# A graph attention pass: the three parts of the queries from one matmul of 192 columns, added by VectorE

## The chip, the cores and the metric

One core of a Trainium2 chip. The metric is the device time of one execution in microseconds; of several, the median. The profile is of one execution, with its own time. Its engines are PE (TensorE), DVE (VectorE), ACT (ScalarE), POOL (GpSimd) and SP (SyncE).

## The reference

A graph of 12500 nodes with 128 features and 412500 edges (200000 random pairs in both directions, and a loop for each node), sorted. Cut to what matters:

```python
q = (X @ Wq)[src]; k = (X @ Wk)[dst]          # 64 columns each
e = jnp.tanh(q + k)
scores = e @ Wphi
exp_scores = jnp.exp(scores - jnp.max(scores))
denom = segment_sum(exp_scores, src)
alpha = exp_scores / (denom[src] + 1e-09)
msg = alpha[:, None] * ((X @ Wy_w + Wy_b)[dst] + e @ We)
out = layernorm(X + segment_sum(msg, src), axis=-1)
```

## The kernel before

The nodes stand in 98 blocks of 128. The first parts of the kernel make a table in HBM with a row per node (64 columns of k, 128 of x), keep the queries of all nodes in SBUF as `q3` (per block three bf16 parts of 64 columns each, whose sum is the f32 query), and sort the edges so that each tile of 128 edges has all its sources in one block. Then comes the main part, in which the change lies, and at the end the normalization.

The main part is one pass over the tiles of edges, 16 to a chunk and four to a step ("quad", `q` in the code); it has 206 chunks, 824 steps. The code of each engine is written out step by step, software-pipelined by hand, with semaphores that count steps. For step q:

- SyncE loads, once a chunk, the numbers of the sources within their block, broadcast to all partitions (L1060, 512 KB); it may be up to two chunks ahead of the one-hots (L1059).
- GpSimd gathers the table rows of the step, four indirect DMAs of 128 rows (L1085), into one of five slots of `gathered`. It waits until the sums of the step five before are made (L1082). Every 72nd step (18 chunks are a "period") is not gathered by it but brought by SyncE, row by row: 512 single-row copies (L1073), 32 in each of 16 chunks of the period, with row numbers read into registers (L1069). Before the first of them SyncE waits for the sums of the last step of the period before (L1067). There are 11 such periods; the last chunks have no such copies.
- VectorE builds once a chunk the one-hots of the sources, transposed (`src_onehots_T`, L1154) and straight (L1157).
- TensorE makes the queries of the step's edges (L1109): the transposed one-hot is the weights, and the three bf16 parts of the block's queries are the moving operand. The three matmuls of a tile add up in PSUM; the four tiles lie side by side in bank 0 or 1 (`QK`), by turns.
- VectorE adds the gathered k (L1168, one instruction for the four tiles) into columns ROW to ROW+A of the slot; ScalarE takes the tanh in place (L1129); VectorE multiplies by phi and reduces (L1176, L1178); ScalarE takes the exponential (L1134) and scales the one-hots with it (L1140).
- TensorE makes the sums of the step (L1120, f32, four matmuls of 193 columns, which the profile shows as eight), three steps behind the queries, into banks 4 to 7; VectorE adds them to the sums of the blocks (L1192, four instructions).

Within one step VectorE's order is: one-hots (every fourth step), L1168 of q-1, L1176 and L1178 of q-2, four L1192 of q-4. TensorE's is: queries of q, sums of q-3. TensorE's queries of step q wait until L1168 of q-2 has read the bank (L1103). A few of the last chunks stand in branches, since their number depends on the data.

Of the kernel before, what the change touches and what calls it, by code (L numbers as in the profile page):

```python
# [4 lines left out]
PARTS = 128  # L5
COLS = 64
UNIT = 16
QUAD = 4
# [24 lines left out]
def gnn_program(nc, x, src, dst, Wq, Wk, Wphi, Wy_w, Wy_b, We, out):  # L33
    f32, i32, u32 = mybir.dt.float32, mybir.dt.int32, mybir.dt.uint32
    bf16, f16 = mybir.dt.bfloat16, mybir.dt.float16
    ALU, ACT, AX = mybir.AluOpType, mybir.ActivationFunctionType, mybir.AxisListType
# [3 lines left out]
    A = Wq.shape[1]  # L40
# [5 lines left out]
    ROW = A + D  # L46
# [37 lines left out]
    def sb(where, name, shape, dt):  # L84
        return where.enter_context(nc.sbuf_tensor(name, shape, dt))

    def sem(name):
        return ctx.enter_context(nc.semaphore(name))

    with ctx:  # L90
        bank = [ctx.enter_context(nc.psum_tensor(f"bank{i}", [PARTS, 512], f32)) for i in range(8)]
# [17 lines left out]
        q3 = sb(ctx, "q_parts", [PARTS, NB * 3 * A], bf16)  # L109
# [11 lines left out]
        def spread(col, n, m):  # L121
            return col.rearrange("p (a m) -> p a m", a=1).to_broadcast([PARTS, n, m])
# [753 lines left out]
        slot = sb(lists, "gathered", [PARTS, RING + 1, QUAD, SLOT], f32)  # L876
# [3 lines left out]
        ohT = sb(lists, "src_onehots_T", [PARTS, 2, CHUNK * PARTS], bf16)  # L880
# [87 lines left out]
        def tensor_lists(e):  # L968
# [3 lines left out]
            for n, i in enumerate(LOADS):  # L972
# [5 lines left out]
                for j in range(min(4, NR - i)):  # L978
# [3 lines left out]
        gathered = [sem(f"gathered_{i}") for i in range(RING)]  # L982
        rows_by_sync = [sem(f"rows_by_sync_{i}") for i in range(4)]
        lows_loaded = [sem(f"src_in_block_rows_loaded_{i}") for i in range(LOB)]
        sums_cleared_vector = sem("sums_cleared_vector")
        onehots_made, onehots_T_made = sem("src_onehots_made"), sem("src_onehots_T_made")
        queried, added_qk, tanh_made = sem("queried"), sem("added_qk"), sem("tanh_made")
        times_phi, scored, weights_made, weighted = sem("times_phi"), sem("scored"), sem("weights_made"), sem("weighted")
        totalled, accumulated = sem("totalled"), sem("accumulated")
# [1 line left out]
        steps_over = {k: sem(f"steps_over_{k}") for k in ENGINES}  # L991
        arrive = {k: sem(f"pass_over_{k}") for k in ENGINES if k != "sync"}
        leave = {k: sem(f"pass_next_{k}") for k in ENGINES if k != "sync"}
        pass_sems = [*gathered, *rows_by_sync, *lows_loaded, sums_cleared_vector, onehots_made, onehots_T_made, queried, added_qk, tanh_made,
                     times_phi, scored, weights_made, weighted, totalled, accumulated, row_max, core_max, shift_made, eps_made, *steps_over.values()]
        QK, SM = [bank[0], bank[1]], [bank[4], bank[5], bank[6], bank[7]]
        H3 = NB * SUMS // 3
        NC = NTS // CHUNK
        SURE = min(NC, -(-NT // CHUNK))
# [16 lines left out]
        def slot_of(q):  # L1016
            return RING if by_sync(q) else pool_no(q) % RING

        def wait_for_rows(e, q):
            if by_sync(q):  # L1020
                e.wait_ge(rows_by_sync[q // PERIOD % 4], 16 * STEP_ROWS * (q // PERIOD // 4 + 1))
            else:
                e.wait_ge(gathered[pool_no(q) % RING], 16 * QUAD * (pool_no(q) // RING + 1))
# [4 lines left out]
        def load_blocks(e, regs, which, t):  # L1028
            p_, c_ = t // MAPC, t % MAPC
            e.load(regs, bmap[p_:p_ + 1, which, c_:c_ + CHUNK])  # L1030
# [63 lines left out]
        def tensor_steps(e, regs, first, end, limit):  # L1094
            for step in range(first, end):
                q = step
                if q < limit:
                    c = q // QUADS_PER_CHUNK
                    if q % QUADS_PER_CHUNK == 0:
                        load_blocks(e, regs, 0, q * QUAD)  # L1100
                    e.wait_ge(onehots_T_made, c + 1)
                    if q >= 2:
                        e.wait_ge(added_qk, q - 1)  # L1103
                    for j in range(QUAD):
                        t = q * QUAD + j
                        o = t % CHUNK * PARTS
                        b = e.snap(regs[t % CHUNK], min_val=0, max_val=(NB - 1) * 3 * A)
                        for s_ in range(3):
                            made = e.matmul(QK[q % 2][:, j * A:(j + 1) * A], ohT[:, c % 2, o:o + PARTS], q3[:, bass.ds(b + s_ * A, A)],  # L1109
                                            start=s_ == 0, stop=s_ == 2)  # L1110
                    made.then_inc(queried, 1)
                q = step - 3
                if 0 <= q < limit:
                    r = slot_of(q)
                    e.wait_ge(weighted, q + 1)
                    if q >= 2:
                        e.wait_ge(accumulated, (q - 1) * QUAD)
                    for j in range(QUAD):
                        o = j % 2 * SUMS
                        made = e.matmul(SM[q % 2 * 2 + j // 2][:, o:o + SUMS], ohw[:, q % 3, j, :], slot[:, r, j, A:SLOT], start=True, stop=True)  # L1120
                    made.then_inc(totalled, 1)
# [21 lines left out]
        def vector_steps(e, regs, first, end, limit):  # L1143
            if first == 0:
                if SURE < NC:
                    e.memset(score[:, SURE * CHUNK:NTS], -1e30)
            for step in range(first, end):
                q = step
                if q < limit and q % QUADS_PER_CHUNK == 0:
                    c = q // QUADS_PER_CHUNK  # L1150
                    e.wait_ge(lows_loaded[c % LOB], 16 * (c // LOB + 1))
                    if c >= 2:
                        e.wait_ge(queried, (c - 1) * QUADS_PER_CHUNK)
                    e.tensor_scalar(ohT[:, c % 2, :], lob[:, c % LOB, :], part0[:, :], None, ALU.is_equal).then_inc(onehots_T_made, 1)  # L1154
                    if c >= 2:
                        e.wait_ge(weighted, (c - 1) * QUADS_PER_CHUNK)
                    e.tensor_tensor(oh[:, c % 2, :, :, :], lo[:, c * CHUNK:(c + 1) * CHUNK].rearrange("p (q a j) -> p q a j", a=1, j=QUAD)  # L1157
                                    .to_broadcast([PARTS, QUADS_PER_CHUNK, PARTS, QUAD]),
                                    row1c[:, :, :].rearrange("p (a n) j -> p a n j", a=1).to_broadcast([PARTS, QUADS_PER_CHUNK, PARTS, QUAD]),
                                    ALU.is_equal).then_inc(onehots_made, 1)  # L1160
                if step < 3:
                    e.memset(sums[:, step * H3:(step + 1) * H3 if step < 2 else NB * SUMS], 0.0).then_inc(sums_cleared_vector, 1)
                q = step - 1
                if 0 <= q < limit:
                    r = slot_of(q)
                    e.wait_ge(queried, q + 1)
                    wait_for_rows(e, q)
                    e.tensor_tensor(slot[:, r, :, ROW:ROW + A], QK[q % 2][:, 0:QUAD * A].rearrange("p (j f) -> p j f", f=A), slot[:, r, :, 0:A],  # L1168
                                    ALU.add).then_inc(added_qk, 1)
                q = step - 2  # L1170
                if 0 <= q < limit:
                    r, k = slot_of(q), q % 2
                    e.wait_ge(tanh_made, q + 1)
                    if q >= 2:
                        e.wait_ge(scored, q - 1)
                    e.tensor_tensor(ephi[:, k], slot[:, r, :, ROW:ROW + A], spread(phi[:, :], QUAD, A), ALU.mult).then_inc(times_phi, 1)  # L1176
                    e.wait_ge(times_phi, q + 1)
                    e.tensor_reduce(score[:, q * QUAD:(q + 1) * QUAD], ephi[:, k], AX.X, ALU.add).then_inc(scored, 1)  # L1178
                q = step - 4
                if 0 <= q < limit:  # L1180
                    if q % QUADS_PER_CHUNK == 0:
                        load_blocks(e, regs, 1, q * QUAD)
                    e.wait_ge(totalled, q + 1)
                    if q == 0:
                        e.wait_ge(sums_cleared_vector, 3)
                    for j in range(QUAD):
                        t = q * QUAD + j
                        o = j % 2 * SUMS
                        b = e.snap(regs[t % CHUNK], min_val=0, max_val=(NB - 1) * SUMS)
                        if t:  # L1190
                            e.wait_ge(accumulated, t)
                        e.tensor_tensor(sums[:, bass.ds(b, SUMS)], sums[:, bass.ds(b, SUMS)], SM[q % 2 * 2 + j // 2][:, o:o + SUMS],  # L1192
                                        ALU.add).then_inc(accumulated, 1)
# [311 lines left out]
```

## Time and profile before

| | us |
|---|---|
| median of 3 runs (lowest, highest) | 7010.81 (7007.23, 7012.87) |
| the profiled execution | 7016.36 |
| its span, first to last instruction | 7014.5 |
| busy: PE, DVE, ACT, POOL | 3898.3, 3592.0, 2751.7, 3447.3 |
| main part, from the first L1109 to the last L1120 | 1326.5 to 6917 |

The mean granted TensorE clock is 0.66 of full speed. In the rows of a timeline, the first number is when the work starts, in us from the span's start, the second how long it takes from the first of the instructions to the end of the last, and in brackets stands how long the engine was idle before it and what ended that. "remote" and "issue" are endings for which the profile shows no instruction of the core.

### The profile page before, as it was taken

To read this page: it belongs to the slowest core of one execution; us is meant where nothing else is said; L and a number is where in the kernel's file an instruction comes from. 1 tells how busy PE (TensorE), PEld (TensorE's weight loads), DVE (VectorE), ACT (ScalarE), POOL (GpSimd) and SP (SyncE) were. 2 spreads that over 40 slices of the span, in tenths; PEclk is the share of its full clock that TensorE was granted. 3 is DMA by queue.
4 is the path that set the end of the run, shared out by engine and by line. 5 is a ranking of instruction groups with operands and counts; after the bars stand their busy time and mean duration, and the time that the engine had idled before them with its cause. 6 is when DMAs were issued, how large, how long until landed. Compare 5 with 4: busy or idle time off the path is not lost. (4 is left out here: it accounts for less than half of the span.)

```text
span 7014.5 us, 115608 instructions
## 1 busy us (share of the span) xinstructions
PE 3898.3 (56%) x25925; PEld 2946.3 (42%) x25925; DVE 3592.0 (51%) x8202; ACT 2751.7 (39%) x10900; POOL 3447.3 (49%) x3516
## 2 busy tenths in 40 slices
PE   7899999554544544544444445445445444454456
PEld 6555555343433433433434334334334334343346
DVE  7788888544444444444444444444444444444446
ACT  3788888322322322323223223223223223232235
POOL 1133323455655555655555555555555555555552
PEclk9766666666666666666666666666666666666668
DMA  2100000222322222222222222222222222222234
GB/s 82 45 4 4 5 4 4 62 75 75 84 74 77 80 75 81 80 74 79 77 76 81 76 75 84 74 78 80 79 80 77 75 79 79 75 82 76 76 91 100
DMA packets 288906, 479.68 MB, mean 68 GB/s; under 512 B 96903, under 2 KB 208745, under 8 KB 287988
## 3 DMA queue, kind: packets, MB, share of 16 engines
q0 software_dynamic: 164032, 321.94, 17.4%
q1 hardware_dynamic: 106418, 145.33, 6.5%
q10 hardware_dynamic: 17794, 4.91, 0.3%
q8 instruction: 253, 4.15, 0.2%
q14 instruction: 409, 3.35, 0.2%
HBM read 456.45 MB, written 20.60 MB: 68 GB/s over the span
## 5 line engine op out<-in xcount | busy, mean ns | idle before, releaser
L1085 POOL DMA_INDIRECT gathered<-table,dst_rows x3252 | 3109.2, 956 | 2496.0 <-PE bank L1120 1167.3
L1120 PE MATMUL bank<-gathered,weighted_onehots 128*128 128x193 f32 x6592 | 1939.8, 437 | 997.1 <-issue 677.5
L1120 PEld LDWEIGHTS bank<-gathered,weighted_onehots 128*128 128x128 f32 x6592 | 1519.4, 257 | 1145.2 <-issue 901.7
L1109 PE MATMUL bank<-q_parts,src_onehots_T 128*128 x9888 | 818.0, 215 | 1996.7 <-DVE src_onehots_T L1154 1460.1
L1129 ACT ACTIVATE gathered<-gathered 128x256 f32<-128x256 f32 x824 | 346.3, 420 | 3597.9 <-DVE gathered L1168 3305.6
L1109 PEld LDWEIGHTS bank<-q_parts,src_onehots_T 128*128 128x128 bf16 x9888 | 686.3, 108 | 2271.3 <-issue 2160.6
L1192 DVE TENSOR_TENSOR block_sums<-block_sums,bank 128x193 f32 x3296 | 1169.2, 355 | 637.5 <-issue 198.9
L1140 ACT ACTIVATE weighted_onehots<-src_onehots,edge_weight 128x128 f32<-128x128 bf16 x3296 | 1075.3, 397 | 26.9
L817 ACT ACTIVATE places_past_far<-bank,stat 128x98 bf16<-128x98 f32 x2727 | 884.7, 400 | 129.3 <-DVE place_col L800 58.1
L1168 DVE TENSOR_TENSOR gathered<-bank,gathered 128x256 f32<-128x256 f32 x824 | 345.8, 420 | 1145.3 <-remote 1124.2
L1154 DVE TENSOR_SCALAR src_onehots_T<-src_in_block_rows,partition_number_from 128x2048 bf16<-128x2048 bf16 x206 | 155.2, 754 | 1335.6 <-DMA src_in_block_rows<-src_in_block_list 1280.5
L859 POOL DMA_INDIRECT sorted_list<-sorted_groups,unit_destinations x248 | 317.1, 1279 | 812.0 <-DVE sorted_groups L787 748.1
L817 ACT ACTIVATION_READ_ACCUMULATOR places_past_far<-bank,stat 128x1 f32 x2727 | 705.7, 265 | 0.0
L842 PE MATMUL bank<-block_onehots,before_far 128*128 128x392 bf16 x806 | 408.5, 507 | 0.0
L849 PE MATMUL bank<-col_records,row_onehots 128*128 128x128 f16 x3223 | 402.7, 298 | 4.2 <-DVE col_records L765 4.2
L849 PEld LDWEIGHTS bank<-col_records,row_onehots 128*128 128x128 bf16 x3223 | 380.6, 124 | 29.9 <-issue 24.8
L1134 ACT ACTIVATE edge_weight<-scores,stat 128x4 f32<-128x4 f32 x824 | 245.0, 297 | 308.6 <-DVE scores L1178 211.0
L1178 DVE TENSOR_REDUCE scores<-e_times_phi 128x4 f32<-128x256 f32 x824 | 346.1, 420 | 28.1
L841 PE MATMUL bank<-base_parts_flat,ones 2*128 2x392 bf16 x806 | 348.1, 432 | 17.1 <-DMA base_parts_flat<-base_parts 14.2
L1176 DVE TENSOR_TENSOR e_times_phi<-gathered,phi 128x256 f32<-128x256 f32 x824 | 347.8, 422 | 0.0
L1157 DVE TENSOR_TENSOR src_onehots<-src_in_block,row_to_quad 128x2048 bf16<-128x2048 bf16 x206 | 250.9, 1218 | 0.0
L760 DVE TENSOR_TENSOR row_onehots<-place_row,row_to_sort_chunk 128x3584 bf16<-128x3584 bf16 (+1 forms) x125 | 233.9, 1872 | 0.0
(182 smaller groups left out, 2021.7 us busy)
## 6 DMA issues: line engine op xcount, KB each, us to landing
src_in_block_rows<-src_in_block_list SPq DMA_DIRECT2D x206, 512.0 KB
gathered<-table SPq DMA_DIRECT2D x5632, 0.8 KB
gathered<-table,dst_rows POOLq DMA_INDIRECT x3252
table<-in_x SPq DMA_DIRECT2D x4, 1562.5 KB
x_in<-in_x SPq DMA_DIRECT2D x24, 256.0 KB, 3.0
x_again<-in_x SPq DMA_DIRECT2D x48, 128.0 KB, 2.3
out<-out_rows SPq DMA_DIRECT2D x48, 128.0 KB, 1.9
sorted_list<-sorted_groups,unit_destinations POOLq DMA_INDIRECT x248
```

Source lines behind the costliest of these rows:

```text
L817: made = e.activation(past_far[:, k % 3, j, :], PL[b % len(PL)][:, j * NB:(j + 1) * NB], ACT.Relu, bias=NEAR, accum_out=pos[:, g % 2, t0 + ...
L841: e.matmul(o, ones[0:2, :], flat[:, g % FLATS, t0:t0 + mt, :], start=True, stop=False)
L842: e.matmul(o, before_far[:, :], hot[:, g % 2, c, h0 // PB, :, 0:mt].rearrange("p b t -> p t b"), start=False, stop=True).then_inc(placed, 1)
L849: made = e.matmul(O[:, 0:2 * COLS], hotr[:, k, t // PB, :, t % PB], recc[:, k, :, t // PB, :, t % PB], start=c + t == 0, stop=c * SORT_CHU ...
L1085: e.indirect_dma_start(slot[:, r, j, 0:ROW], None, table, bass.IndirectOffsetOnAxis(ap=gidx[:, t:t + 1].bitcast(u32), axis=0)).then_inc(ga ...
L1109: made = e.matmul(QK[q % 2][:, j * A:(j + 1) * A], ohT[:, c % 2, o:o + PARTS], q3[:, bass.ds(b + s_ * A, A)], start=s_ == 0, stop=s_ == 2)
L1120: made = e.matmul(SM[q % 2 * 2 + j // 2][:, o:o + SUMS], ohw[:, q % 3, j, :], slot[:, r, j, A:SLOT], start=True, stop=True)
L1129: e.activation(slot[:, r, :, ROW:ROW + A], slot[:, r, :, ROW:ROW + A], ACT.Tanh).then_inc(tanh_made, 1)
L1140: made = e.activation(ohw[:, q % 3, j, :], oh[:, c % 2, q % QUADS_PER_CHUNK, :, j], ACT.Copy, scale=wexp[:, q % 3, j:j + 1])
L1176: e.tensor_tensor(ephi[:, k], slot[:, r, :, ROW:ROW + A], spread(phi[:, :], QUAD, A), ALU.mult).then_inc(times_phi, 1)
L1178: e.tensor_reduce(score[:, q * QUAD:(q + 1) * QUAD], ephi[:, k], AX.X, ALU.add).then_inc(scored, 1)
L1192: e.tensor_tensor(sums[:, bass.ds(b, SUMS)], sums[:, bass.ds(b, SUMS)], SM[q % 2 * 2 + j // 2][:, o:o + SUMS], ALU.add).then_inc(accumulat ...
```

## The change

Per tile one matmul of 192 columns now writes the three parts side by side in PSUM, two tiles to a bank, so a step takes two banks and the two turns take banks 0 to 3. Where VectorE had one add (PSUM and k from SBUF), it now has two reductions, one for each bank, that add the three parts of two tiles into the slot's columns ROW to ROW+A, a wait for the second of them, and an add of k in place, both inputs in SBUF. Banks 2 and 3 were not used in the main part before. All other lines are as they were.

```diff
-        QK, SM = [bank[0], bank[1]], [bank[4], bank[5], bank[6], bank[7]]
+        QK, SM = [[bank[0], bank[1]], [bank[2], bank[3]]], [bank[4], bank[5], bank[6], bank[7]]
...
-                        for s_ in range(3):
-                            made = e.matmul(QK[q % 2][:, j * A:(j + 1) * A], ohT[:, c % 2, o:o + PARTS], q3[:, bass.ds(b + s_ * A, A)],
-                                            start=s_ == 0, stop=s_ == 2)
+                        made = e.matmul(QK[q % 2][j // 2][:, j % 2 * 3 * A:(j % 2 + 1) * 3 * A], ohT[:, c % 2, o:o + PARTS], q3[:, bass.ds(b, 3 * A)],
+                                        start=True, stop=True)
                     made.then_inc(queried, 1)
...
                     wait_for_rows(e, q)
-                    e.tensor_tensor(slot[:, r, :, ROW:ROW + A], QK[q % 2][:, 0:QUAD * A].rearrange("p (j f) -> p j f", f=A), slot[:, r, :, 0:A],
-                                    ALU.add).then_inc(added_qk, 1)
+                    for h in range(2):
+                        made = e.tensor_reduce(slot[:, r, 2 * h:2 * h + 2, ROW:ROW + A], QK[q % 2][h][:, 0:6 * A].rearrange("p (j s f) -> p j f s", s=3, f=A),
+                                               AX.X, ALU.add)
+                    made.then_inc(query_summed, 1)
+                    e.wait_ge(query_summed, q + 1)
+                    e.tensor_tensor(slot[:, r, :, ROW:ROW + A], slot[:, r, :, ROW:ROW + A], slot[:, r, :, 0:A], ALU.add).then_inc(added_qk, 1)
```

## Rows read from the trace of the kernel before

**Rows 1.** SyncE's timeline at the start of two periods and at the last copies.

```profile
2306.68 5.47 SPq L1060 DMA_DIRECT2D src_in_block_rows<-src_in_block_list  x3
...
2329.56 29.14 SPq L1073 DMA_DIRECT2D gathered<-table  x32
...
2800.97 4.94 SPq L1060 DMA_DIRECT2D src_in_block_rows<-src_in_block_list  x3
...
6691.80 27.89 SPq L1073 DMA_DIRECT2D gathered<-table  x32
```

**Rows 2.** Waits from 1400 to 6800: who <- for whom, total us, times, longest.

```profile
DVE src_onehots_T L1154 <- DMA src_in_block_rows<-src_in_block_list: 1276.0, 154, 15.8
...
DVE gathered L1168 <- remote: 1081.6, 200, 7.1
...
SPq L1069 <- remote: 97.7, 6, 16.4
...
SPq L1069 <- PE bank L1120: 65.2, 4, 16.4
```

**Rows 3.** SyncE's timeline in two short stretches, without and with gathers beside it.

```profile
3989.82 3.10 SPq L1073 DMA_DIRECT2D gathered<-table  x8
...
4000.71 13.64 SPq L1073 DMA_DIRECT2D gathered<-table  x13
```

**Rows 4.** Groups by line: count, busy us, mean ns; then idle before.

```profile
L1178 DVE TENSOR_REDUCE scores<-e_times_phi 128x4 f32<-128x256 f32 x824 | 346.1, 420 | 28.1
...
L1192 DVE TENSOR_TENSOR block_sums<-block_sums,bank 128x193 f32 x3296 | 1169.2, 355 | 637.5 <-issue 198.9
```

**Rows 5.** VectorE's timeline: a chunk that begins a period, and two late steps.

```profile
2311.05 0.75 DVE L1154 TENSOR_SCALAR src_onehots_T<-src_in_block_rows,partition_number_from 128x2048 bf16<-128x2048 bf16 x1 [9.66 <-DMA src_in_block_rows<-src_in_block_list]
...
2316.93 0.43 DVE L1168 TENSOR_TENSOR gathered<-bank,gathered 128x256 f32<-128x256 f32 x1
2317.28 0.42 DVE L1176 TENSOR_TENSOR e_times_phi<-gathered,phi 128x256 f32<-128x256 f32 x1
2317.73 0.42 DVE L1178 TENSOR_REDUCE scores<-e_times_phi 128x4 f32<-128x256 f32 x1
...
2327.45 0.42 DVE L1168 TENSOR_TENSOR gathered<-bank,gathered 128x256 f32<-128x256 f32 x1 [4.72 <-remote]
...
2330.96 1.22 DVE L1157 TENSOR_TENSOR src_onehots<-src_in_block,row_to_quad 128x2048 bf16<-128x2048 bf16 x1
...
6761.16 0.42 DVE L1168 TENSOR_TENSOR gathered<-bank,gathered 128x256 f32<-128x256 f32 x1 [5.68 <-remote]
...
6908.25 0.42 DVE L1168 TENSOR_TENSOR gathered<-bank,gathered 128x256 f32<-128x256 f32 x1 [4.99 <-issue]
```

**Rows 6.** TensorE's timeline: its first and a later step of that chunk.

```profile
2311.95 1.74 PE L1109 MATMUL bank<-q_parts,src_onehots_T 128*128 x12 [12.54 <-DVE src_onehots_T L1154]
2313.59 2.91 PE L1120 MATMUL bank<-gathered,weighted_onehots 128*128 128x193 f32 x8
...
2320.02 1.55 PE L1120 MATMUL bank<-gathered,weighted_onehots 128*128 128x193 f32 x8 [0.82 <-DVE block_sums L1192]
```

**Rows 7.** GpSimd's timeline in that chunk.

```profile
2316.77 0.94 POOL L1085 DMA_INDIRECT gathered<-table,dst_rows  x1 [8.32 <-PE bank L1120]
...
2331.47 1.53 POOL L1085 DMA_INDIRECT gathered<-table,dst_rows  x1 [0.30 <-issue]
```

**Rows 8.** Stretches of 3 us: PE, PEld, DVE, ACT, POOL busy (count); granted clock; DMA.

```profile
3992.00:3995.00 3.00, 3.00 (x16) 2.83 (x17) 1.66 (x5) 1.67 (x6) 0.00 (x0) 0.50 0.01 2
...
3998.00:4001.00 3.00, 2.06 (x20) 1.87 (x20) 2.56 (x8) 1.87 (x6) 2.39 (x3) 1.00 0.35 95
...
4010.00:4013.00 3.00, 0.00 (x0) 0.00 (x0) 0.00 (x0) 0.00 (x0) 2.24 (x3) 0.50 0.29 81
```

**Rows 9.** The instructions of line L1109: TensorE's register operations.

```profile
L1109 PEldq FUSED_REGOPS  x6592: 4/46/744, 1326.6 to 6896.6; - x200
```

**Rows 10.** The page's first line.

```profile
span 7014.5 us, 115608 instructions
```

More of the change, by code:

```diff
@@ L986, in gnn_program @@
         onehots_made, onehots_T_made = sem("src_onehots_made"), sem("src_onehots_T_made")
+        query_summed = sem("query_summed")
         queried, added_qk, tanh_made = sem("queried"), sem("added_qk"), sem("tanh_made")
@@ L993, in gnn_program @@
         leave = {k: sem(f"pass_next_{k}") for k in ENGINES if k != "sync"}
-        pass_sems = [*gathered, *rows_by_sync, *lows_loaded, sums_cleared_vector, onehots_made, onehots_T_made, queried, added_qk, tanh_made,
+        pass_sems = [*gathered, *rows_by_sync, *lows_loaded, sums_cleared_vector, onehots_made, onehots_T_made, query_summed, queried, added_qk, tanh_made,
                      times_phi, scored, weights_made, weighted, totalled, accumulated, row_max, core_max, shift_made, eps_made, *steps_over.values()]
-        QK, SM = [bank[0], bank[1]], [bank[4], bank[5], bank[6], bank[7]]
+        QK, SM = [[bank[0], bank[1]], [bank[2], bank[3]]], [bank[4], bank[5], bank[6], bank[7]]
         H3 = NB * SUMS // 3
```

## The prediction

> **What bounds the kernel now.** The main part is a pass over 206 chunks of 16 tiles (four steps of four tiles). I read SyncE's timeline first, since it is the one queue without gaps: it issues 32 single-row copies in 27.89 us, then one load of a chunk's low numbers (L1060), then the next 32 [rows 1]. A chunk takes as long as that with the load between: 29.5 us in the mean of the period below. The list of waits says the same from the other side: between 1400 and 6800 the one-hot build of L1154 waited 1276.0 us in 154 times for the load that stands behind those copies in SyncE's queue, 8.3 us each [rows 2]. SyncE is slow because of the gathers beside it: 8 copies took 3.10 us while no gather ran (0.39 us each), 13 took 13.64 us while GpSimd gathered (1.05 each) [rows 3].
>
> A period is 18 chunks, 16 of them with copies. One begins at 2306.68 and the next at 2800.97, 494.3 us, of which SyncE spends 22.9 us (to 2329.56) on three loads and on a wait, and the other 471.4 us (16 x 29.5) copying [rows 1]. The wait, for the sums of the last period, is 162.9 us in ten times, 16.3 us each [rows 2]. After 6719.7 no copies are left [rows 1], and the last eight chunks run at the pace of gathers and compute. So the path to the end is: SyncE's copies in 11 periods, ten waits of 16.3 us, eight free chunks, a short drain.
>
> **The change part by part.**
>
> *VectorE.* The add of L1168 is replaced by two reductions of 384 elements to 128 from PSUM, a wait for the second, and an add of 256 from SBUF. No row has such a reduction. The nearest are L1178, 256 elements in 420 ns, and L1192, 193 in 355 ns [rows 4]: 65 ns for 63 elements, so 384 take about 420 + 128 x 1.03 = 552 ns. Instructions that follow each other start 0.07 to 0.08 us before the earlier one ends (L1168 at 2316.93 lasts 0.43, L1176 starts 0.35 later); where one waits for the one before, it is 0.45 for 0.42 [rows 5]. So the first reduction takes 0.47, the second with the wait 0.59, and the add costs what it cost: +1.06 us a step, 4.24 us a chunk, 824 x 1.06 = 873 us in all. The element stride of 64 in the reduction's input may cost more: at double the time per element it is +1.85 us a step; if both reductions cost only what L1178 does, +0.8. I take 1.06, from the row of the same operation.
>
> Where does it fall? In a chunk of SyncE's pace VectorE waits 8.3 us for the load and 1081.6 / 200 = 5.4 us before one L1168 [rows 2], 13.7 us together, three times what is added. Even the chunk at the start of a period, from the one-hot build at 2311.05 to 2330.30 (where L1154 comes again, 0.66 before L1157), has 4.72 us idle in 19.3, before an L1168 [rows 5]. Its other 14.5 us become 18.8, still under 19.3. A load is also issued up to two chunks ahead at that place, so what one chunk lags isn't passed to SyncE. Behind the new wait are queued L1176, L1178 and four L1192, and ScalarE's tanh waits for the add; all of these come 1.06 us later and into the same idle time.
>
> *TensorE.* Per tile three weight loads, three matmuls of 64 columns and three register operations become one of each with 192 columns. Columns are the same. In the first step of a chunk the twelve took 1.74 us, 0.145 each, and the sums behind them start when they end [rows 6]. Four of 192 columns at the same granted clock should take between 4 x 0.145 = 0.6 and 1.0 us: 0.8 us saved, in the later steps 0.1 to 0.3. This stands on a path: GpSimd's gathers resume at 2316.77 on the end of those sums, 8.32 us idle before, and SyncE's wait ended about 2328.3, a good microsecond of register load before its first copy at 2329.56, so 11.5 us behind them [rows 1, 7]. The sums that SyncE's wait names had been made by then: they are the matmuls at 2320.02, over at 2321.57 [rows 6]. What holds SyncE for the other 6.7 us the trace calls remote; it is fixed to the start of the gathers. So the wait gets 0.8 us shorter if that holds, ten times: -8 us. If SyncE followed the sums instead, three VectorE steps would push them by 3.2 us less the 0.8, still 4.3 us before its release; only where the held time is added on top does it cost 10 x 2.4 = +24. Range -9 to +24, taken -5.
>
> *The last eight chunks.* Nothing waits for SyncE there. VectorE was idle 5.68 us before the L1168 at 6761.16 [rows 5], against 4.24 added: it fits, with 1.4 us to spare. Bounds: 0, and 8 x 4.24 = +34 if that idle time can't be used. I take +5, near the lower end, because a chunk has the idle time in its rows.
>
> *Drain.* The last L1168 is at 6908.25 [rows 5]; behind it all is serial, one added sequence, +1 us. The first chunk: SyncE's copies start without it, 0.
>
> *PSUM.* Banks 2 and 3 were unused in this pass, so no new wait for a bank; L1103's wait for added_qk is as before and comes two steps later.
>
> *Sum*: -5 + 5 + 1 = +1 us. The profiled execution took 7016.36 us (span 7014.5, 1.9 around it), so 7017; it lay 5.6 us above the median of the three, so against 7010.81 the forecast is **7012 us**.
>
> **Rules weighed.** The new add has both inputs in SBUF, where L1168 had one in PSUM. Rows first: the gather at 2316.77 ran with L1176 beside it (two SBUF inputs, 2317.28) and took 0.94 us; the one at 2331.47 ran beside L1157 (1.22 us, also two) and took 1.53 [rows 5, 7]. The Trainium skill (SBUF — State Buffer, Who interferes with whom) says that a VectorE instruction with two SBUF inputs contends with a GpSimd instruction that reads SBUF, and that one with a single SBUF input does not. By that rule the change slows gathers; by the row of L1176, an instruction of the new add's very shape, it costs nothing. I go with the row, and keep the rule as a rival.
>
> The granted clock: a chunk's first sums took 2.91 us, the third ones 1.55 [rows 6]; in the chunk at 3989 the clock at the same places is 0.50 and 1.00, so 1.2 and 2.4 GHz, and 0.50 where TensorE has nothing to do [rows 8]. The Trainium skill (TensorE: Matmul & The Clock Gate, Part 1) says that the clock is throttled by default and that activity releases it. By that rule fewer matmuls may leave later sums at the low level.
>
> **Rivals.**
>
> *A. VectorE or its lag decides where no copies run (slower).* For it: VectorE, GpSimd and SyncE all stood still until about 2328 though the rows of that step were gathered before GpSimd's pause of 8.32 us; if this is a hold on all queues and no slack, added work comes on top. The eight last chunks become 4.24 us longer (+34) and the SyncE wait 2.4 (+24), with 1 for the drain: +59, 7070. It decides from the point where VectorE's work and the hold together pass the 20 us of a chunk's gathers (16 of 0.94 with 0.30 between them [rows 7]). Against it: at 6761 the hold ends just when rows of the gather before it may have landed, which is slack.
>
> *B. Gathers are slowed by the new add.* 0.59 us (1.53 - 0.94) on the four gathers a chunk that have such an add beside them is 2.4 us; hidden under SyncE's copies, except in the last eight chunks: +19 on the sum above, 7031. Against: the row of L1176.
>
> *C. The clock stays low.* 2.91 - 1.55 = 1.36 us on two of four sums a chunk: hidden as well but for the last eight, +22, 7034. For it: only the first two groups of sums pay it now, and each step has 0.3 to 1 us less TensorE work. Against: the sums are the larger part and stay.
>
> *D. SyncE gets faster (faster).* TensorE drops 13,184 matmuls and loads and 6592 register operations [rows 9], 17% of 115608 instructions [rows 10]. If SyncE's slow copies (0.39 us alone, 0.87 in the mean of 32) are slow because all queues fetch and issue at once, part of it comes back. All 5632 copies (11 x 512) lose about 0.48 us each against the fast ones (27.89 / 32 less 0.39). A tenth of the 17% of that is 46 us, 6966. Against: from 4010 to 4013 TensorE, VectorE and ScalarE did nothing at all [rows 8], and the 13 slow copies run from 4000.71 to 4014.35. That the change doesn't do what it says can't be: 19,776 instructions go.
>
> **Chances.** Within 0.2% (14 us) is what a measurement of this kernel can't tell from no change. The forecast 0.60, with its own range 6998 to 7026 (0.51 inside 14 us, 0.03 below, 0.06 above); A 0.18 (0.16 above, 0.02 within); B and C together 0.12 (0.10 above, 0.02 within); D 0.10, below. Sums: faster 0.13, same 0.55, slower 0.32. The range goes to 6990 below, leaving out most of D, and to 7065 above, leaving out the far half of A: 0.8 stays.
>
> **What would show it.** Two reductions of about 550 ns and an add of 420 a step, VectorE busy some 870 us more; its wait for the load in a copy chunk down from 8.3 to about 4 us; four matmuls in 0.6 to 1.0 us behind the one-hot build; 32 copies in the same 27 us; SyncE's ten waits at 15.5 us; the last L1168 at most 195 us behind the last copy (now 188.6). Wrong if periods differ from 491 us by over 3 us, if those waits grow, if L1154 no longer waits for its load, or if a gather beside the new add takes over 1.1 us.

## The result, and the profile after

| | us |
|---|---|
| before, median of 4 (lowest, highest) | 7009.02 (6986.53, 7012.87) |
| after, median of 4 (lowest, highest) | 6690.17 (6660.70, 6719.41) |
| the profiled execution of after, its span | 6685.31, 6683.5 |

The ratio is 0.9551 [0.9504, 0.9598]: 4.5% faster. The forecast was 7012 us, the range 6990 to 7065.

The page of after says first that the sum for VectorE was right: busy 3592.0 us before, 4416.4 now, +824 for the predicted 873. VectorE's new instructions cost what was forecast, and still the kernel is faster: something else changed. The new page's first lines and the groups of the main part (busy us, mean ns, then the idle time before):

```profile
span 6683.5 us, 97481 instructions
...
PE 3650.0 (55%) x19333; PEld 2725.9 (41%) x19333; DVE 4416.4 (66%) x9850; ACT 2747.7 (41%) x10900; POOL 3483.1 (52%) x3516
...
L1086 POOL DMA_INDIRECT gathered<-table,dst_rows x3252 | 3142.7, 966 | 2124.4 <-issue 935.0
```

115,608 instructions have become 97,481 [rows 10]. SyncE's timeline, the loads at the start of two neighbouring periods and the first copies of each, answers to [rows 1]:

```profile
2255.59 5.36 SPq L1061 DMA_DIRECT2D src_in_block_rows<-src_in_block_list  x3
2274.27 25.91 SPq L1074 DMA_DIRECT2D gathered<-table  x32
...
2714.03 5.62 SPq L1061 DMA_DIRECT2D src_in_block_rows<-src_in_block_list  x3
2735.81 28.45 SPq L1074 DMA_DIRECT2D gathered<-table  x32
...
3990.17 24.70 SPq L1074 DMA_DIRECT2D gathered<-table  x32
4014.91 0.36 SPq L1061 DMA_DIRECT2D src_in_block_rows<-src_in_block_list  x1
4016.68 23.52 SPq L1074 DMA_DIRECT2D gathered<-table  x32
```

This period takes 2714.03 - 2255.59 = 458.4 us; the one of [rows 1] took 494.3. All eleven together, by the one-hot builds of L1154, take 5399 us before and 5067 after. These 332 us are the whole difference of the two profiled executions (331). In the chunks in the middle of a period 32 copies take 26.6 us before and 24.2 now (medians, from the start of the first to the start of the last). The copies did not all get faster by the same share. Of the 5456 distances between neighbouring copies of a run of 32, the quickest quarter is at 0.42 us or less in both; those over 1.2 us were 1547, in all 2858 us, and are 1313, in all 2503 us. Two stretches of the trace of after: in the first GpSimd gathers, with one pause of 1.82 us, in the second it stands still from 4018.4 on.

```profile
3999.99 14.87 SPq L1074 DMA_DIRECT2D gathered<-table  x14
...
4016.68 6.63 SPq L1074 DMA_DIRECT2D gathered<-table  x12
```

The first takes 1.06 us a copy (1.05 in [rows 3]), the second 0.55. So there still are stretches as slow as that of before, but in the mean a kind of stretch that hardly seems TensorE's affair got faster: from the last instruction of TensorE, VectorE and ScalarE in a chunk to the next L1154, while only GpSimd gathers, neighbouring copies start 0.86 us apart before (1021 distances) and 0.66 after (1299).

Waits from 1400 to 6800, answering to [rows 2]:

```profile
DVE src_onehots_T L1154 <- DMA src_in_block_rows<-src_in_block_list: 1215.2, 153, 16.7
...
DVE gathered L1169 <- remote: 21.4, 8, 4.6
...
SPq L1070 <- PE bank L1120: 94.4, 7, 15.6
...
SPq L1070 <- remote: 14.8, 1, 14.8
```

VectorE still waits 7.9 us a time for its load (8.3 before), so SyncE still sets the chunk. The other wait, 1081.6 us in 200 times, is gone from its place. TensorE had a wait like it, which no row shown so far has: in the fourth step of a chunk its sums stood still between matmuls, for nothing that the profile shows ("issue"). One such step of the kernel before, and TensorE's waits of this kind before and after:

```profile
4002.87 0.32 PE L1120 MATMUL bank<-gathered,weighted_onehots 128*128 128x193 f32 x1 [0.79 <-issue]
...
4004.32 0.48 PE L1120 MATMUL bank<-gathered,weighted_onehots 128*128 128x193 f32 x1 [1.13 <-issue]
...
4006.42 1.12 PE L1120 MATMUL bank<-gathered,weighted_onehots 128*128 128x193 f32 x3 [1.62 <-issue]
```

```profile
PE bank L1120 <- issue: 657.3, 645, 2.5
```

```profile
PE bank L1120 <- issue: 81.3, 55, 4.9
```

The eight matmuls of that step took 6.3 us before, from the first to the end of the last, and take 1.55 now (medians). In those microseconds SyncE's copies were slow too: three from 4000.7 to 4006.4. VectorE and TensorE in one chunk of after, answering to [rows 5, 6]:

```profile
4018.81 0.75 DVE L1154 TENSOR_SCALAR src_onehots_T<-src_in_block_rows,partition_number_from 128x2048 bf16<-128x2048 bf16 x1 [7.85 <-DMA src_in_block_rows<-src_in_block_list]
...
4020.62 1.02 DVE L1169 TENSOR_REDUCE gathered<-bank 128x128 f32<-128x384 f32 x2
4021.67 0.43 DVE L1173 TENSOR_TENSOR gathered<-gathered 128x256 f32<-128x256 f32 x1
...
4029.47 1.02 DVE L1169 TENSOR_REDUCE gathered<-bank 128x128 f32<-128x384 f32 x2
...
4033.38 1.01 DVE L1169 TENSOR_REDUCE gathered<-bank 128x128 f32<-128x384 f32 x2
```

```profile
4019.70 0.82 PE L1109 MATMUL bank<-q_parts,src_onehots_T 128*128 x4 [9.59 <-DVE src_onehots_T L1154]
4020.32 2.89 PE L1120 MATMUL bank<-gathered,weighted_onehots 128*128 128x193 f32 x8
...
4033.61 1.54 PE L1120 MATMUL bank<-gathered,weighted_onehots 128*128 128x193 f32 x8 [1.16 <-DVE block_sums L1196]
```

Steps follow each other at 3.9 us there, without a pause before the fourth. Both clock levels are seen in the sums as before, 2.89 and 1.54 us.

### The profile page after: what moved, and what is told of

It is laid out like the page before. It is cut to its first block and busy times, and to the rows that moved or that the text cites. A ratio compares the mean times of both kernels' runs of the same rounds, so it can differ in the third digit from the quotient of the medians.

```text
span 6683.5 us, 97481 instructions
## 1 busy us (share of the span) xinstructions
PE 3650.0 (55%) x19333; PEld 2725.9 (41%) x19333; DVE 4416.4 (66%) x9850; ACT 2747.7 (41%) x10900; POOL 3483.1 (52%) x3516
## 3 DMA queue, kind: packets, MB, share of 16 engines
q0 software_dynamic: 164032, 321.94, 18.4%
## 5 line engine op out<-in xcount | busy, mean ns | idle before, releaser
L1086 POOL DMA_INDIRECT gathered<-table,dst_rows x3252 | 3142.7, 966 | 2124.4 <-issue 935.0
L1120 PE MATMUL bank<-gathered,weighted_onehots 128*128 128x193 f32 x6592 | 1874.9, 448 | 949.5 <-DVE block_sums L1196 716.7
L1120 PEld LDWEIGHTS bank<-gathered,weighted_onehots 128*128 128x128 f32 x6592 | 1573.8, 266 | 1115.8 <-issue 732.4
L1109 PE MATMUL bank<-q_parts,src_onehots_T 128*128 x3296 | 624.0, 328 | 1961.3 <-DVE src_onehots_T L1154 984.9
L1109 PEld LDWEIGHTS bank<-q_parts,src_onehots_T 128*128 128x128 bf16 x3296 | 401.1, 123 | 2186.0 <-issue 2142.9
L1154 DVE TENSOR_SCALAR src_onehots_T<-src_in_block_rows,partition_number_from 128x2048 bf16<-128x2048 bf16 x206 | 158.5, 769 | 1279.8 <-DMA src_in_block_rows<-src_in_block_list 1219.2
L1169 DVE TENSOR_REDUCE gathered<-bank 128x128 f32<-128x384 f32 x1648 | 836.9, 550 | 55.0 <-DMA gathered<-table,dst_rows 21.8
L1173 DVE TENSOR_TENSOR gathered<-gathered 128x256 f32<-128x256 f32 x824 | 351.1, 426 | 28.2
L1157 DVE TENSOR_TENSOR src_onehots<-src_in_block,row_to_quad 128x2048 bf16<-128x2048 bf16 x206 | 250.7, 1217 | 0.0
```

The costliest lines, as they stand in the source:

```text
L1086: e.indirect_dma_start(slot[:, r, j, 0:ROW], None, table, bass.IndirectOffsetOnAxis(ap=gidx[:, t:t + 1].bitcast(u32), axis=0)).then_inc(ga ...
L1109: made = e.matmul(QK[q % 2][j // 2][:, j % 2 * 3 * A:(j % 2 + 1) * 3 * A], ohT[:, c % 2, o:o + PARTS], q3[:, bass.ds(b, 3 * A)], start=Tru ...
L1169: made = e.tensor_reduce(slot[:, r, 2 * h:2 * h + 2, ROW:ROW + A], QK[q % 2][h][:, 0:6 * A].rearrange("p (j s f) -> p j f s", s=3, f=A), A ...
L1173: e.tensor_tensor(slot[:, r, :, ROW:ROW + A], slot[:, r, :, ROW:ROW + A], slot[:, r, :, 0:A], ALU.add).then_inc(added_qk, 1)
```

## The experiments

Two theories. **T**: TensorE's dropped instructions (rival D of the prediction) let SyncE copy faster. **V**: VectorE's longer steps do it, since they spread the work of a chunk. A third, **R**, is that TensorE's register operations alone do it. Runs with the same letter ran on one chip (g and h on the same), and the chips differed more than the kernels, so each ratio is to the kernel before on that chip: 7126.19 us beside f1 to f4, and 5547.08 (e), 5551.43 (g), 5547.59 (h) and 5549.16 (k). The expectations of e1 to e4 are for a chip on which the kernel before takes 7010 us, and it took 5547.

### Where the kernel before takes 7126 us

f1_changed is the changed kernel.

> The changed kernel itself, beside the kernel before. Where the kernel before takes about 7010 us (32 row copies in 26.6 us): 6690. Where it takes about 5547 (32 copies in 14.6 us, gathers set the pace): if the gathers are what VectorE's new instructions slow, 3252 gathers x 0.046 us = 150 us more, 5690; if TensorE's instructions count there, less, 5650.

Measured: 6775.49, 0.951 [0.9477, 0.9543].

f2_one_part is the kernel before with only the first of the three parts; it leaves out two thirds of each query sum, and drops TensorE's 19,776 instructions without VectorE's additions.

```diff
-                        for s_ in range(3):
+                        for s_ in range(1):
...
-                                            start=s_ == 0, stop=s_ == 2)
+                                            start=True, stop=True)
```

> Again the kernel before with the first query part alone (two thirds of the query sum left out), to see it where copies are slow. At 7010 us of the kernel before: theory T (TensorE's instructions) 6550 to 6720, theory V (VectorE's pace) 7000 to 7015. At 5547: 5543 as measured.

Measured: 6682.36, 0.9379 [0.9346, 0.9413].

f3_vector_only is the changed kernel with three matmuls of 64 columns per tile side by side in place of the one: VectorE as after, TensorE's instructions as many as before.

```diff
-                        made = e.matmul(QK[q % 2][j // 2][:, j % 2 * 3 * A:(j % 2 + 1) * 3 * A], ohT[:, c % 2, o:o + PARTS], q3[:, bass.ds(b, 3 * A)],
-                                        start=True, stop=True)
+                        for s_ in range(3):
+                            made = e.matmul(QK[q % 2][j // 2][:, (j % 2 * 3 + s_) * A:(j % 2 * 3 + s_ + 1) * A], ohT[:, c % 2, o:o + PARTS],
+                                            q3[:, bass.ds(b + s_ * A, A)], start=True, stop=True)
```

> Again the changed kernel with three matmuls per tile side by side. At 7010 us of the kernel before: T 7010 to 7070, V 6660 to 6720. At 5547: 5690 as measured.

Measured: 7042.42, 0.9885 [0.9849, 0.992].

f4_no_copies is the kernel before in which GpSimd gathers all 824 steps and SyncE copies nothing.

```diff
-            return q // PERIOD < NSP and q % PERIOD == PERIOD - 1
+            return False
...
-            return q - min(q // PERIOD, NSP)
+            return q
...
-                if i < NSP:
+                if False:
```

> The kernel before with GpSimd gathering all 824 steps, no row copies; same output. At 7010 us of the kernel before: if the copies set the pace there, 206 chunks at 22.0 us as in its last seven, so about 6000. At 5547: 44 gathers more at 1.25 us each, 55 us, 5602.

Measured: 6321.76, 0.8873 [0.8841, 0.8905].

SyncE's timelines of f1, f2 and f3, one run of 32 copies each:

```profile
4001.56 24.69 SPq L1074 DMA_DIRECT2D gathered<-table  x32
```

```profile
4014.38 24.27 SPq L1073 DMA_DIRECT2D gathered<-table  x32
```

```profile
4030.97 27.77 SPq L1074 DMA_DIRECT2D gathered<-table  x32
```

The medians of the steady chunks are 24.7, 24.4 and 26.6 us, the periods 469, 460 and 492 in the mean. f1 and f3 issue the same VectorE work and differ only in TensorE's 19,776 instructions: 7042 - 6775 = 267 us, of which 255 lie in the periods (5417 against 5162 us). f2 has the drop alone and gets 444 us. f2 and f3 both lie where T put them and not where V did. So T is shown, by two pairs: TensorE's smaller query work lets SyncE copy faster. The effect outlasts that work: between the last instruction of TensorE, VectorE and ScalarE in a chunk and the next L1154, with only GpSimd gathering, copies start in the mean 1.02 us apart in f3, 0.67 in f1 and 0.57 in f2.

What T's gain is made of is not shown. The dropped instructions also took time: TensorE's query matmuls were busy 1104.9 us in f3, 621.8 in f1 and 353.6 in f2, and no run changes the number without the time.

V is worth 84 us by itself, 1.2% (a profile of the kernel before on that chip is lacking, so where they lie isn't known). f1 stands 6775 - 6682 = 93 us over f2; it has VectorE's added work and also the columns of the two parts that f2 leaves out. The wait before L1168 needed both to go: with VectorE's work alone (f3) 569.4 us in 192 times are left of it, and with TensorE's drop alone (f2) a wait of 764.5 us in 203 times stands before L1192 in its place.

f4 shows what these copies cost here: without them the chunk is 23.7 us and the kernel 11% faster. The 6000 us expected were missed, since they counted on chunks of 22.0 us. 23.7 is still over the pace of the gathers, and GpSimd's timeline of f4 says why:

```profile
4001.11 0.94 POOL L1085 DMA_INDIRECT gathered<-table,dst_rows  x1 [2.15 <-remote]
...
4010.08 0.94 POOL L1085 DMA_INDIRECT gathered<-table,dst_rows  x1 [0.30 <-issue]
4012.90 0.94 POOL L1085 DMA_INDIRECT gathered<-table,dst_rows  x1 [1.88 <-remote]
```

Eight gathers, then some 2 us held by nothing that the core's instructions show, 347 times between 1400 and 6800 (706.8 us). So a chunk of 16 takes 2 x 11.8 = 23.6 us instead of 16 x 1.25 = 20.

### Where the kernel before takes 5547 us

The same edits, with one more: e3_static_parts reads the parts at a fixed block, so that TensorE keeps its 9888 loads and matmuls of the query sum and drops its register operations; it leaves out the choice of the block. e4 is the changed kernel with the edit of f4.

```diff
-                                            q3[:, bass.ds(b + s_ * A, A)],
+                                            q3[:, s_ * A:(s_ + 1) * A],
```

> The kernel before with only the first of the three query parts (it leaves out two thirds of the query sum): per tile one weight load, one matmul of 64 columns, one register operation; VectorE as before. Theory T (TensorE's instructions: all queues and the landings behind them are slowed by the number of instructions issued in the burst behind the one-hots): 6550 to 6720 us, 32 row copies in at most 24.5 us, no stall of 5 us before an L1168. Theory V (VectorE's slower steps spread the burst out): 7000 to 7015, copies in 26.6 us, the stall stays. Theory D as I forecast (nothing matters but GpSimd): 7010.

> The changed kernel, but with three matmuls of 64 columns each per tile, not added in PSUM but side by side in the same two banks: TensorE's instructions as before, VectorE's as after; same output. T: 7010 or more, up to 7070, with the stall and 26.6 us for 32 copies. V: 6660 to 6720 like the changed kernel.

> The kernel before with the query parts read at a fixed place (always block 0; it leaves out the choice of the block): no register operations and no register addresses in the 9888 query matmuls, their number and VectorE as before. If the register operations and addresses are what TensorE's part of the gain is made of: near 6690. If it is the number of instructions of any kind: 6592 + 3296 of 19776 gone, half the gain, 6850. If it is the matmuls and loads: 7010. V: 7010.

> The changed kernel with GpSimd gathering all 824 steps and no row copies by SyncE; same output. If SyncE's copies set the pace of 16 of 18 chunks: 206 chunks at the 21.6 us of the last seven of the changed kernel, 4450 us in place of 5218, so about 5900. If the pace is set by something that the copies only share in (gathers or landings): over 6500.

| | us | ratio |
|---|---|---|
| e1_one_part | 5542.58 | 0.9985 [0.9974, 0.9997] |
| e2_vector_only | 5690.46 | 1.0258 [1.0218, 1.0297] |
| e3_static_parts | 5542.18 | 0.9998 [0.9985, 1.001] |
| e4_changed_no_copies | 5756.72 | 1.0377 [1.0347, 1.0407] |

No theory has its gain here: neither TensorE's drop (e1) nor its register operations (e3) nor VectorE's spreading (e2) makes the kernel faster, beyond 0.15%. The cost of VectorE's work is left. e4 can't decide its question here, since GpSimd sets the pace with SyncE's copies and without them. SyncE's and GpSimd's timelines of e3, which takes the time of the kernel before:

```profile
4002.06 14.81 SPq L1073 DMA_DIRECT2D gathered<-table  x32
```

```profile
4002.65 0.94 POOL L1085 DMA_INDIRECT gathered<-table,dst_rows  x1 [0.30 <-issue]
4003.91 0.95 POOL L1085 DMA_INDIRECT gathered<-table,dst_rows  x1 [0.31 <-issue]
```

32 copies take 14.8 us beside gathers that never stop, one each 1.25 us; "remote" stands before none of them. The chunk is 16 x 1.25 = 20 us (20.1 by the builds of L1154): GpSimd's gathers bound the kernel, SyncE waits, and nothing that relieves SyncE can show. What slows a gather does. GpSimd's group in e1 and in e2, from 1500 to 5400:

```profile
L1085 POOL DMA_INDIRECT gathered<-table,dst_rows x3096 | 2955.5, 955 | 944.6 <-issue 942.4 <-PE bank L1120 2.1
```

```profile
L1086 POOL DMA_INDIRECT gathered<-table,dst_rows x2987 | 2991.7, 1002 | 910.2 <-issue 882.2 <-PE bank L1121 28.0
```

47 ns on each of 3252 gathers is 153 us; e2 stood 148 us over e1. So VectorE's added work slows the gathers, as rival B said. What I had read against it, one row of a gather beside L1176, was true and not enough: the mean over all gathers is what counts.

The traces also show which gathers got longer. One with nothing beside it takes 945 ns. Over that, the 3252 gathers take 32 us more in e1 and 183 in e2, which is 151 us of difference. 104 of them fall on the 410 gathers that have the one-hot build L1158 beside them: 1261 ns in the mean, against 1008 beside the same instruction in e1 (L1157, 408 gathers). Both kernels have that build; the longer steps only bring it together with the gathers at another point. The other 47 us fall on gathers beside the new add or the multiplication behind it (L1174, L1181). A gather with nothing but a reduction L1170 beside it takes 945 ns as well (371 of them).

By the rule weighed in the prediction (the Trainium skill, SBUF — State Buffer, Who interferes with whom) the new add contends with GpSimd's reads. The trace agrees for gathers that start while it runs, 1037 ns in the mean of 514 in e2. But that is the smaller part of the price.

g1 is the changed kernel there, and g2 asks whether any queue's instructions count.

> The changed kernel, as what the others of this call stand against. Theory T (TensorE's fewer instructions relieve the queues where these are slow, VectorE's part costs where gathers set the pace): 0.951 of the kernel before where that takes 7010 to 7130 us; where it takes about 5547 us, 1.026 (VectorE's part alone gave 1.0258 there, one part alone 0.9985), about 5690 us. Rival V (VectorE's slower steps make the gain): under 1.0 on either.

Measured: 5698.21, 1.0252 [1.0225, 1.0278]. **The change that gains 4.9% on the chip of f1 loses 2.5% on this one.** Its rows of GpSimd and VectorE at a chunk's start show how the build lengthens a gather:

```profile
4011.20 1.53 POOL L1086 DMA_INDIRECT gathered<-table,dst_rows  x1 [0.30 <-issue]
```

```profile
4010.69 1.22 DVE L1157 TENSOR_TENSOR src_onehots<-src_in_block,row_to_quad 128x2048 bf16<-128x2048 bf16 x1
4011.83 1.01 DVE L1169 TENSOR_REDUCE gathered<-bank 128x128 f32<-128x384 f32 x2
```

The gather starts 0.51 us into L1157 and takes 1.53 us. 154 gathers of g1 start at that point of the build, 0.45 to 0.6 us into it, and 7 of e1's.

g2_signals_on_act adds to the changed kernel 24 signals a step on ScalarE's queue (12 behind the tanh, 12 behind the weighted one-hots), 19,776 in all, 17 ns each:

```diff
+                    for _ in range(12):
+                        e.sem_inc(counted, 1)
```

> The changed kernel, with 24 additions to an otherwise unused semaphore per step on ScalarE's queue: 19,776 instructions more, as many as TensorE lost by the change, but on another queue and without work. Theory N (the number of instructions of all queues together is what slows SyncE's copies and the steps where the kernel before takes 7010 to 7130 us): nearly all of the gain is gone, 0.99 to 1.00 of the kernel before, 32 copies again in 26.6 us. Theory P (only TensorE's loads, matmuls and their register operations count): within 0.5% of the changed kernel, 0.951 to 0.956, 32 copies in 24.2 to 24.7 us. Where the kernel before takes about 5547 us: both say the time of the changed kernel, within 0.5%, unless ScalarE's steps get too long (2.4 us of work per step now, steps of 4 us).

> The kernel before with the q parts read at a fixed block, so that TensorE's queue loses its register operations and address loads (some 10,000 of its instructions) but keeps every load and matmul; leaves out the choice of the block. Where the kernel before takes 7010 to 7130 us: if every instruction of TensorE's queue counts alike, half of what one part gave with its 19,800 (0.938), so 0.965 to 0.970; if only loads and matmuls count, 0.99 to 1.00; if only the register operations count, 0.90 to 0.94, since more of them go than there. Where it takes about 5547 us: 1.00 again.

> The changed kernel with GpSimd gathering all 824 steps and no copies by SyncE; same output. Where the kernel before takes 7010 to 7130 us: the kernel before without copies gave 0.887. If the fewer instructions of TensorE help the gathers and landings too, 0.84 to 0.87 here; if they help SyncE's copies alone, VectorE's slower steps are left over: 0.89 to 0.91, slower than the kernel before without copies. Where it takes about 5547 us: 1.038 again.

Measured, g2 to g4: 1.0261 [1.023, 1.0292], 0.9992 [0.9976, 1.0009], 1.0359 [1.0332, 1.0387]. These edits decide something only where SyncE sets the pace, and here it doesn't. The same holds for h1, h2 and h3, the same three edits again:

> The changed kernel with 24 additions to an otherwise unused semaphore per step on ScalarE's queue, as before (there, where the kernel before took 5551 us, it was 1.0261 beside 1.0252 of the changed kernel: no cost). Where the kernel before takes 7010 to 7130 us, the changed kernel is 0.951 to 0.955 of it. Theory N (instructions of any queue count): 0.99 to 1.00, 32 copies in 26.6 us. Theory P (TensorE's own only): 0.951 to 0.96, 32 copies in 24.2 to 24.7 us. Where it takes about 5550 us: 1.026 again.

> The kernel before with the q parts read at a fixed block: TensorE loses 9888 register operations, one for each matmul of the query part, and keeps its 9888 loads and matmuls; leaves out the choice of the block. Where the kernel before takes 7010 to 7130 us: if every instruction of TensorE's queue counts alike, half of what one part gave with its 19,800 (0.938), so 0.965 to 0.970; if only loads and matmuls count, 0.99 to 1.00; if only the register operations count, 0.90 to 0.94. Where it takes about 5550 us: 1.00 again.

> The changed kernel with GpSimd gathering all 824 steps and no copies by SyncE; same output. Where the kernel before takes 7010 to 7130 us: the kernel before without copies gave 0.887. If the fewer instructions of TensorE help the gathers and landings too, 0.84 to 0.87 here; if they help SyncE's copies alone, VectorE's slower steps are left over: 0.89 to 0.91. Where it takes about 5550 us: 1.037 again.

Measured, h1 to h3: 1.0254 [1.0236, 1.0271], 0.999 [0.9977, 1.0003], 1.0387 [1.0363, 1.041]. Two of them ran a last time, beside the edit of f4 on the kernel before:

> The changed kernel with 24 additions to an otherwise unused semaphore per step on ScalarE's queue. Where the kernel before takes 7010 to 7130 us (the changed kernel is 0.951 to 0.955 of it): instructions of any queue count: 0.99 to 1.00; TensorE's own only: 0.951 to 0.96. Where it takes about 5550 us: 1.026 again, as twice before.

> The kernel before with the q parts read at a fixed block: TensorE loses 9888 register operations and keeps its loads and matmuls; leaves out the choice of the block. Where the kernel before takes 7010 to 7130 us: every instruction of TensorE's queue counts alike: 0.965 to 0.970; only loads and matmuls: 0.99 to 1.00; only the register operations: 0.90 to 0.94. Where it takes about 5550 us: 1.00 again.

> The kernel before with GpSimd gathering all 824 steps and no copies by SyncE; same output. Where the kernel before takes 7010 to 7130 us: 0.887, as measured. Where it takes about 5550 us and GpSimd's gathers set the pace, each chunk has 16 gathers either way and 11 chunks' worth of steps (11 steps of 4 gathers at 1.25 us, 55 us) come on top: 1.01; the changed kernel without copies stood 0.011 over the changed kernel there.

Measured, k1 and k2: 1.0247 [1.0222, 1.0272], 0.9989 [0.9979, 0.9998], and k3: 1.008 [1.0056, 1.0103]. Each is what was expected for a chip of this kind, on which the theories agree. So three questions stay open: R, whether another queue's instructions would do what TensorE's do, and whether TensorE's drop also helps where SyncE copies nothing. k3 completes f4: the kernel before without SyncE's copies is 0.887 of it on the one chip and 1.008 on the other. Of the kernels with the full output that ran there it is the fastest on the one (0.951 for the changed kernel). On the other it is 1.7% faster than the changed kernel, but the kernel before itself is the fastest; the changed kernel without copies, 1.036 to 1.039, is the slowest there.

## Why the prediction was wrong

**The step that failed** is the first: "SyncE is slow because of the gathers beside it", and from it 32 copies in the same 27 us. Gathers are one condition (0.39 against 1.05 us a copy), TensorE's query work is another; I found the first and took it for the whole. 32 copies went from 26.6 to 24.2 us. In the sum the copies' change stood at nothing; the term is rival D's, which the prediction had, with a chance of 0.10, and sized at 46 us. The periods, with VectorE's part in them, got 332 us shorter, and TensorE's drop by itself (f1 against f3, f2 against the kernel before) is worth 267 to 444 us. The sizing had no row under it: "a tenth of the 17%".

**The argument that talked it away** was one stretch of 3 us in which the other engines did nothing and SyncE was slow all the same [rows 8]. It took for granted that TensorE can slow SyncE only while it works. In the runs, copies in stretches where only GpSimd works stand 0.86 us apart before and 0.66 after, and 1.02 and 0.67 in f3 and f1: what TensorE issued in the chunk still counts when it has stopped. What carries it over isn't known. The trace of before had a sign of it that the prediction did not weigh: TensorE's own matmuls stood 657.3 us for nothing that the profile shows, beside slow copies.

**VectorE.** Right in size: a pair of reductions in 1.02 us, 550 ns each for 552, +824 us for +873. That it costs nothing on that chip is right only in part: alone it gains 84 us there (f3), and f1 stands 93 us over f2. The idle 5.4 us before L1168 was called slack, rival A called it a hold. It took in added work as slack does (569.4 us left of 1081.6 in f3), and the rest went with TensorE's drop (21.4 us left in the changed kernel).

**TensorE.** Right: four matmuls in 0.82 us. The wait at the period's start was to be 15.5 us, from 16.3, and was 13.7 (94.4 + 14.8 in eight times). This and the first chunks of a period belong to the same -332.

**The last chunks.** +5 was forecast. By the last seven builds of L1154 they take 151.3 us, 154.2 before. The bound of +34 lay far off.

**Rival B** was right that the gathers get slower, and right in its mechanism for about a third of it: the add and the multiplication make 47 of 151 us, the one-hot build 104. Under SyncE's copies its price is small (mean gather 966 for 956 ns). It decides where GpSimd sets the pace, and that differs here from chip to chip, not from stretch to stretch of the kernel.

**Rival C** was right that more sums would run at the low clock level, and right that it would be hidden. Of the 6592 matmuls of the sums 2847 took over 500 ns before and 3522 after; the third step's sums went from 1.92 to 2.66 us (medians). The groups of L1120, before and after:

```profile
L1120 PE MATMUL bank<-gathered,weighted_onehots 128*128 128x193 f32 x6592 | 1939.8, 437 | 997.1 <-issue 677.5
```

```profile
L1120 PE MATMUL bank<-gathered,weighted_onehots 128*128 128x193 f32 x6592 | 1874.9, 448 | 949.5 <-DVE block_sums L1196 716.7
```

11 ns on each is 73 us of TensorE's work, with no slower kernel. The mean granted clock of the whole execution rose all the same, 0.66 to 0.686; no run tested why.

**Rival A** fell: the kernel got faster, and the last eight chunks, which A put at +34 us, did not get longer.

**The chances.** D had 0.10. The working had shown that 471 of a period's 494 us hang on SyncE's rate, and that the change drops a sixth of all instructions. With so much of the time on one rate whose cause wasn't known, an estimate for what moves it should have been bounded from rows (471 us for 16 chunks, against the 20 us that a chunk's gathers take: 151 us a period, over 1600 in eleven) and the range carried down with it.

## What to carry to other kernels

Where the path hangs on the rate of one queue and that rate isn't explained by its own work, treat a change of the other queues' work as a possible change of the path, and bound it by the queue's fastest rate in the trace. A stretch in which the other engines are idle is no proof against it. And before a gain is kept, know which resource bounds the kernel on the chip at hand: here the same two kernels stand at 0.951 and at 1.025, since on one chip SyncE's copies set the chunk and on the other GpSimd's gathers do. And where one engine sets the pace, look at what runs beside each of its instructions: a longer step can cost by moving an old instruction against them.

## What the runs showed of the hardware

- One program took 7009 to 7126 us in two of the comparisons and 5547 to 5551 in the four others, each group within 2%. The part ahead of L1109 takes the same (first L1109 at 1330.6 in the profile after, at 1327.5 in g1, the same kernel). Of the 988 us by which these two differ, 986 lie between the first and the last L1154. The chips of e, of f, of g and h, and of k were each seen at one speed only, and for the first comparison the chip isn't on record. So whether the speed belongs to the chip or to its state at the time isn't shown.
- In that part, on the slower ones, a gather waits some 2 us after each eight (f4: 347 waits for "remote", 706.8 us; none in k3, the same kernel), and a run of 32 copies takes 0.87 us for each (27.89 / 32 in [rows 1]), 0.46 on the others (14.81 / 32). The packets themselves are not slower: in the same kernel the gathers' queue kept its DMA engines busy for 18.4% of 6683.5 us there (after, 1230 us), and for 21.7% of 5695.0 (g1, 1236). So the difference isn't in the DMA engines' time for the packets; where it lies is not settled.
- There, 19,776 instructions fewer on TensorE's queue gave 267 to 444 us, that is 13.5 to 22.5 ns for each, though TensorE's matmuls took only 56% of the span. Copies got faster even while TensorE was idle (1.02 us apart in f3, 0.67 in f1).
- A gather that starts while VectorE builds the one-hots L1157, 0.45 to 0.6 us into its 1.2 us, takes 1.53 us in place of 0.945 (g1, 154 times). Beside a reduction from PSUM alone it takes 0.945.
- ScalarE's queue takes 19,776 additional signals at no cost where the gathers set the pace (5696.6 beside 5698.21).

The DMA rows of the page of after and of g1:

```profile
q0 software_dynamic: 164032, 321.94, 18.4%
```

```profile
q0 software_dynamic: 164032, 321.94, 21.7%
```
